# Latent attention row maxima: the causal mask is added by VectorE's maximum instruction instead of by a TensorE product

## What is computed

```
scores = jnp.einsum('bhqd,bhkd->bhqk', q, k) / jnp.sqrt(jnp.float32(HEAD_DIM))
causal = jnp.tril(jnp.ones((t, t), dtype=bool))
scores = jnp.where(causal[None, None], scores, -jnp.inf)
attn = jax.nn.softmax(scores, axis=-1)
out = jnp.einsum('bhqk,bhkd->bhqd', attn, v)
```

## Time and profile before

| | |
|---|---|
| median of 3 runs | 1852.05 us (1848.89 to 1857.47) |
| the profiled execution's own time | 1852.1 us |
| its span | 1850.1 us |
| granted TensorE clock, mean | 0.952 |
| busy: PE, PEld, DVE, ACT, POOL | 1637.9, 1064.1, 1316.3, 961.0, 822.9 us |

### The profile page before, as it was taken

How to read it: one execution, slowest core, us unless ns; L and a number is a source line. 1 busy time by engine, 2 the same in 40 slices (tenths; PEclk the granted TensorE clock), 3 DMA queues, 4 the chain that set the end, 5 groups by cost and what they waited for, 6 DMA issues and landing times. The chain is left out here.

```text
span 1850.1 us, 44114 instructions
## 1 busy us (share of the span) xinstructions
PE 1637.9 (89%) x16808; PEld 1064.1 (58%) x16808; DVE 1316.3 (71%) x3530; ACT 961.0 (52%) x2513; POOL 822.9 (44%) x827
## 2 busy tenths in 40 slices
PE   6587788998999988899899999999889998898787
PEld 3464457465765656556575656656565566655443
DVE  4754577768868778677777778787787678786373
ACT  3435443575445753467445754457544764456324
POOL 5508562564426534365436545266435553453000
PEclk9799899999999988999999999999999999999788
DMA  7210212203320032101222033100232013300030
GB/s 250 62 36 18 66 30 70 70 5 71 97 54 19 10 84 79 53 22 33 58 79 70 5 71 97 54 19 22 67 84 59 16 33 102 82 19 5 9 85 7
DMA packets 160002, 100.56 MB, mean 54 GB/s; under 512 B 59160, under 2 KB 147352, under 8 KB 159512
## 3 DMA queue, kind: packets, MB, share of 16 engines
q1 hardware_dynamic: 159504, 96.94, 19.8%
q10 hardware_dynamic: 288, 0.81, 0.1%
HBM read 55.36 MB, written 27.28 MB: 45 GB/s over the span
## 5 line engine op out<-in xcount | busy, mean ns | idle before, releaser
L1345 ACT ACTIVATE shared<-bank 128x512 f32<-128x512 f32 (+1 forms) x384 | 201.5, 531 | 208.5 <-PE bank L1052 205.8
L1646 DVE TENSOR_REDUCE nmx<-bank 128x1 f32<-128x512 f32 (+3 forms) x352 | 222.8, 638 | 90.0 <-PE bank L1024 87.8
L1837 POOL TENSOR_TENSOR soft<-soft,prec 128x512 f32<-128x512 f32 x128 | 131.9, 1040 | 341.6 <-DVE prec L1478 341.4
L1245 ACT ACTIVATE soft<-bank,nmax 128x128 f32<-128x128 f32 x512 | 179.7, 379 | 88.8 <-DVE nmax L1470 87.9
L1799 POOL TENSOR_TENSOR qk_rs<-qk_rs,minus_half 128x16 f32<-128x16 f32 x64 | 187.5, 2929 | 5.3
L697 PE MATMUL bank<-w_sb,hT 128*128 128x512 f32 x256 | 136.7, 624 | 7.3 <-DVE rot L1460 3.8
L1052 PE MATMUL bank<-shared 75*128 75x384 bf16 (+3 forms) x512 | 142.2, 306 | 0.0
L1051 PE MATMUL bank<-b_sb 128*128 128x128 bf16 x512 | 114.4, 225 | 20.2 <-ACT shared L1345 17.4
L665 PE MATMUL bank<-c_sb,soft 128*128 128x128 f32 x608 | 102.8, 301 | 29.7 <-POOL soft L1837 20.2
L1024 PE MATMUL bank<-shared 72*128 72x256 bf16 (+3 forms) x512 | 127.4, 301 | 0.0
L1254 ACT ACTIVATE soft<-bank 128x512 f32<-128x512 f32 x128 | 74.6, 605 | 75.5 <-PE bank L665 74.8
(11 more groups left out here) (254 smaller groups left out, 4345.2 us busy)
## 6 DMA issues: line engine op xcount, KB each, us to landing
shared<-parts_dram SPq DMA_DIRECT2D x64, 288.0 KB
vm<-v_f SPq DMA_DIRECT2D x112, 128.0 KB, 2.4
parts_dram<-parts SPq DMA_DIRECT2D x96, 128.0 KB, 2.4
L_dram<-the SPq DMA_DIRECT2D x32, 256.0 KB, 2.3
shared<-Z_dram SPq DMA_DIRECT2D x32, 256.0 KB, 3.5
shared<-L_dram SPq DMA_DIRECT2D x32, 256.0 KB, 4.5
shared<-X_dram SPq DMA_DIRECT2D x32, 256.0 KB, 4.8
w_sb<-weights SPq DMA_DIRECT2D x1, 4167.0 KB, 17.1
```

Of the source, the lines that this page charges most:

```text
L1245: a = af(v4(p_sb, 2, 4)[:, j, g], place("fS", j)[:, g * P:(g + 1) * P], ACT.Exp, bias=nmax[:, at:at + 1], accum_out=psums[:, at:at + 1])
L1345: af(v4(PTm, 2, GROUP)[:, u % 2, i, 0:n], place("mST", b, i)[:, 0:n], ACT.Exp).then_inc(mexp_done, 1)
L1646: reduce(v3(nmx[:], HM)[:, h:h + len(heads), c], v3(place("mS", b, t)[:, 0:len(heads) * (c + 1) * P], len(heads)), AX, ALU.max, negate=Tru ...
L1837: tt(p, p, spread(prec[:, at:at + NPAIR], P), ALU.mult).then_inc(fnorm_done, 1)
```

## The change

On PE the mask product is gone, and each score product starts its part of the bank. The constant `causal` becomes 4 x 128 columns wide: 384 columns of zeros and then the mask, so that its last w columns are the mask of a tile of w keys. On DVE each head's part is one `tensor_tensor_reduce`: it adds scores and mask, multiplies by -1, writes the result back over the scores in PSUM, and keeps the minimum of it per row, which is the negated maximum. So a tile of two heads has two instructions, and a tile of four has four. Because `b_sb` grows by 384 bf16 columns, the row parameters that are needed only at the start (`qs`, `ks`) now arrive in `acc`, by a transfer of their own.

```diff
-BF_LAYOUT = [("identb", P), ("near", P), ("far", P), ("far0", P), ("causal", P), ("causalT", P),
+BF_LAYOUT = [("identb", P), ("near", P), ("far", P), ("far0", P), ("causal", 4 * P), ("causalT", P),
...
-         "causal": np.where(j <= i, 0, NEG), "causalT": np.where(i <= j, 0, NEG),
+         "causal": np.concatenate([np.zeros((P, 3 * P)), np.where(j <= i, 0, NEG)], 1), "causalT": np.where(i <= j, 0, NEG),
...
-    R_AT, R_N = offsets([("norm_w", DV), ("qs", DEPTH * DF), ("ks", DEPTH * DF), ("gate_b", NE), ("b2", D)])
+    R_AT, R_N = offsets([("qs", DEPTH * DF), ("ks", DEPTH * DF), ("norm_w", DV), ("gate_b", NE), ("b2", D)])
...
         def R(name):
             a, n = R_AT[name]
-            return r_sb[:, a:a + n]
+            early = R_AT["norm_w"][0]
+            return acc[:, a:a + n] if a < early else r_sb[:, a - early:a - early + n]
...
-                act.dma_start(r_sb[:], rows.to_broadcast([P, R_N])).then_inc(setup_loads, 16)
+                early_r = R_AT["norm_w"][0]
+                act.dma_start(acc[:, 0:early_r], rows[:, 0:early_r].to_broadcast([P, early_r])).then_inc(setup_loads, 16)
+                act.dma_start(r_sb[:], rows[:, early_r:].to_broadcast([P, R_N - early_r])).then_inc(setup_loads, 16)
...
-                    mm(ps[:, :, c * P:w], B("identb"), repeat(B("causal"), len(heads)), start=True, stop=False, skip_group_check=True)
                     for i, h in enumerate(heads):
                         h += GROUP * g
                         m = mm(ps[:, i], Qst[0:9 * DM, h * T + c * P:h * T + w], Kst[0:9 * DM, h * T:h * T + w],
-                               start=False, stop=True, skip_group_check=True)
+                               start=True, stop=True, skip_group_check=True)
...
-                    h = GROUP * g + heads[0]
-                    reduce(v3(nmx[:], HM)[:, h:h + len(heads), c], v3(place("mS", b, t)[:, 0:len(heads) * (c + 1) * P], len(heads)),
-                           AX, ALU.max, negate=True).then_inc(nmx_done, 1)
+                    w = (c + 1) * P
+                    ps = v3(place("mS", b, t)[:, 0:len(heads) * w], len(heads))
+                    for i, h in enumerate(heads):
+                        at = (GROUP * g + h) * NT + c
+                        m = nc.vector.tensor_tensor_reduce(ps[:, i], ps[:, i], B("causal")[:, 4 * P - w:4 * P], -1.0, 3e38,
+                                                           ALU.add, ALU.min, nmx[:, at:at + 1])
+                    m.then_inc(nmx_done, 1)
```

More of the change, by code:

```diff
@@ L294, in sb @@
             return ctx.enter_context(nc.sbuf_tensor(name, [P, n], dt))
-        w_sb, c_sb, b_sb, r_sb = sb("w_sb", W_N), sb("c_sb", C_N), sb("b_sb", B_N, BF16), sb("r_sb", R_N)
+        w_sb, c_sb, b_sb, r_sb = sb("w_sb", W_N), sb("c_sb", C_N), sb("b_sb", B_N, BF16), sb("r_sb", R_N - R_AT["norm_w"][0])
         def W(name):
@@ L673, in hT_ @@
                     else:
-                        pe.wait_ge(setup_loads, 48)
+                        pe.wait_ge(setup_loads, 64)
                     transposes(place("hT"), lambda i: v3(hn_tm, NT)[:, i]).then_inc(head_psum, 1)
@@ L1418, in tables @@
                 def tables():
-                    dve.wait_ge(setup_loads, 48)
+                    dve.wait_ge(setup_loads, 64)
                     for l in range(DEPTH):
@@ L2018, in pack @@
     packed = np.ascontiguousarray(np.concatenate([w[n] for n, _ in weight_layout()], 1))
-    rows = np.concatenate([a["L0_attn_norm_w"], a["L0_ffn_q_scale"].reshape(-1), a["L0_ffn_k_scale"].reshape(-1),
+    rows = np.concatenate([a["L0_ffn_q_scale"].reshape(-1), a["L0_ffn_k_scale"].reshape(-1), a["L0_attn_norm_w"],
                            a["L1_ffn_gate_b"], a["L0_ffn_b2"][DEPTH - 1]])[None]
```

## The result

The changed kernel takes 1860.91 us, the kernel before 1854.59 us (medians of 20 runs each); the ratio is 1.0034, 95% interval 1.0021 to 1.0047. So it is slower by 6.3 us. The time is 4 us above the forecast of 1857; the three runs shown before the prediction had given 1852.05 for the kernel before. The mean granted TensorE clock over the 20 executions of the changed kernel is 0.948; for the kernel before only that of the profiled execution is on record here, 0.952.

The account below looks back on a forecast made before the run. The prediction took PE as the fullest engine, though not alone, with DVE's added work costing in smaller part. From 1852.05 us, -16.4 + 21 + 0.8 = +5.4 gave 1857 us, range 1832 to 1888.

Parts of the forecast that it names:

- near balance: Likeliest case for the whole kernel: PE's gain and DVE's cost nearly cancel, 1843 to 1861 us, chance 0.35.
- TensorE's term: Mask products removed from PE: 27.8 us of work, of which 59% comes back as time, -16.4 us.
- More instructions on VectorE: One instruction per head on DVE, 16 per group: 0.61 us more per group, 19.5 us over 32 groups.
- The accumulator read: Fetching each of 512 minima on DVE: 0.10 us each, 51 us in all (0 to 113).
- VectorE's share: Part of DVE's added 70.5 us that lies on the path: 30%, between 19% and 41%, giving +21 us.
- The write into PSUM: DVE writing to the bank it reads: assumed to cost no rate.
- The start: Larger constants, wider cast and one more small transfer at the kernel's beginning: +0.8 us.
- The last batch: DVE's tiles run nearly back to back there; removing the mask product buys nothing, DVE's addition costs 9 us at most.
- PE as the bound: Rival at the mask products: PE's time comes back and the read is cheap, 1827 to 1845 us, chance 0.27.
- The dear read: Rival on DVE: the accumulator read costs as much as on ACT, 0.19 us; 1861 to 1890 us, chance 0.33.
- The halved rate: Rival on DVE: reading and writing one PSUM bank halves the rate; 1905 us or above, chance 0.05.
- Expected signs: In the profile after: waits for the maximum above 82.8 us, more `nmx` in the chain, means near 0.68, 0.55, 0.42, 0.29 us.

Follow-up runs that it names:

- mask_add: Changed kernel with the mask product kept on PE, so DVE adds the mask a second time; ratio 1.0061 to the kernel before.
- no_mask_reduce: Changed kernel with the plain reduce of before, no mask product, queries scaled down by 100; ratio 0.9960 to the kernel before.
- mask_twice: Kernel before with every mask product issued twice, 27.8 us more TensorE work; ratio 1.0079 to the kernel before.
- mask_reduce: Changed kernel with mask product and reduce of before, so only the changed start is left; ratio 1.0007 to the kernel before.
- one_add: Changed kernel with one new instruction per tile, 352 in place of 512, queries scaled down by 100; ratio 0.9967 to the kernel before.
- early_signal: one_add plus unread reduces over 64, 64 and 256 columns behind the signals of tiles 8, 9 and 10; ratio 1.0010 to the kernel before.
- dve_plus_one: Kernel before plus reduces over 64, 64 and 256 constant columns behind the signals of tiles 8 to 10, 19 us; ratio 1.0012.
- dve_plus_two: Kernel before with each reduce of dve_plus_one added twice, 38 us more VectorE work; ratio 1.0045 to the kernel before.
- split_last_batch: Changed kernel with one instruction per tile in batches 0 to 6, per head only in the last, queries scaled down by 100; ratio 0.9948.
- The three corners: The changed kernel with one or both halves undone: no_mask_reduce (0.9960), mask_add (1.0061) and mask_reduce (1.0007), against the kernel before.

## Why the prediction came out as it did

**The forecast.** +5.4 us near balance, measured +6.3. The case that I called likeliest occurred, but its terms didn't have their sizes, and that the sum fits is luck: PE's gain was put some 8 us too large, and DVE's cost, +21, 7 to 11 us too large (10.0 us in mask_add, 13.7 in the changed kernel over no_mask_reduce). Within DVE's cost a read that costs nothing stood for +15 us and the share of the other work was too low.

**TensorE's term.** The distances were right: mask_twice's rows repeat them. The share was mis-sized: 59% (-16.4 us) was forecast, 31% (-8.7 us) came. I had read the share off the tiles at which PE did not wait for the maximum. That share itself was read from idle weight loads for the most part (115 of the 144 places), and it counts only the first wait: time freed at the other tiles can be lost again further on. The trace of no_mask_reduce has 13 us more idle time on PE than that of mask_reduce, over many waits; which of them takes the 8 us that the forecast counted on isn't shown.

**More instructions on VectorE.** 19.5 us forecast, some 19 us by the distances after. Right, and one_add against the changed kernel shows that this is the term that decides.

**The accumulator read.** 51 us forecast (0 to 113), and nothing occupied; the truth lay at the lower end. The neighbours that I had chosen, ACT's pair and a tiny DVE instruction, both misled: the read doesn't delay its neighbour, except one of its own kind by 0.04 us. What the Trainium skill says in "VectorE: DVE Perf Modes", section "Two Vector instructions with no wait between them", held: two records per instruction. The estimate of 38 us by the Trainium skill's 75 ns per instruction ("Vector Engine (DVE) Microarchitecture Reference", section 5.2) was too high like my 51, since the trace shows no such time for the read. What the read costs is 0.06 to 0.07 us of lateness per signal, and one_add shows that as no time.

**VectorE's share.** 30% was forecast. mask_add gives 10.0 us for some 19 us, about a half; early_signal 8 for 19; but dve_plus_one 2 for 19 and dve_plus_two 8.3 for 38. So it isn't one number: it is higher in early_signal, where PE's work is gone, and in mask_add, where the work stands ahead of the signal, than in dve_plus_one. Of the forecast's +21, 30% of the read's 51 us, +15, was wrong; 30% of the 19.5 us, +6, should have been +10 to +14.

**The write into PSUM** costs 10 ns per instruction, the assumption held. **The start**: +0.8 forecast, 1.5 us later in the trace, 0.0007 in mask_reduce, which can't be told from either. **The last batch**: DVE's part there was put at 9 us at most; split_last_batch shows none of it by its ratio and some 2.5 us at equal clock. The rows of the last batch show DVE nearly back to back, as forecast.

**The rivals.** PE as the bound fell with no_mask_reduce. The dear read fell with one_add and the distances; the measured 1860.9 lies at the edge of its range, 1861 to 1890, but not for its reason. The halved rate fell with the means of 694 and 565 ns. Expected signs: the waits for the maximum grew, as forecast, the chain moved to DVE, and the means for two and four heads were 445 and 322 ns where I had put 420 and 290.

**Open.** The three corners sum to less (-0.47 + 0.54 + 0.07 = 0.14%) than the 0.34% measured; the uncertainties of the corners, some 0.2% each, cover this. At equal clock the sum is +4.5 us and the changed kernel +2.8, which differ by less than their uncertainty. In the corner with the mask product the DVE half costs 0.54%, while dve_plus_one, the same amount of work behind the signals, costs 0.12% on nearly the same kernel; at equal clock they are 11.3 and 4.1 us, still apart. Without the mask product early_signal costs 7.7 us of its own, and lateness adds nothing. Whether lateness matters with the mask product and not without isn't shown: no run moves the signal there.

## What to carry to other kernels

Price both sides of a swap between engines by what each engine's time is worth there, and measure it once by adding work: here 27.8 us of TensorE returned 25% to 31% when removed, though the engine is "89% busy". Differences of a few us are read with the granted clock beside them: here 0.003 of it goes with 3.4 us, as much as the whole change at equal clock. When a fused instruction keeps one result per instruction, count the instructions that a batched one is split into before all else: here the 160 extra ones cost 9 to 12 us and the fusion itself nothing that could be measured.

## What the runs showed of the hardware that wasn't expected

The accumulator read of VectorE has a record of 141 ns, and the next instruction, if it is ready, starts with it (distance 0.00 us); only another accumulating instruction is slowed, by 0.04 us (0.65 against 0.61 us from start to start at 512 columns). On ACT the same kind of read took some 0.19 us of the engine, by the prediction's estimate from the earlier trace rows. An instruction that reads and rewrites one PSUM bank runs at the rate of a reduce, 694 against 684 ns at 512 columns. Repeated executions of one kernel differ mostly with the mean granted clock, 1.14 us for each 0.001.
